# A transformer block on one core: tiles split straight from PSUM, shifts added apart, new orders, and the FFN gating on ScalarE and GpSimd

## The chip, the cores and the metric

The kernel runs on one core of a Trainium2 chip. The metric is the device time of one execution in microseconds. TensorE (PE), VectorE (DVE), ScalarE (ACT) and GpSimd (POOL) work from lists of instructions of their own and wait for each other by semaphores. All loads and stores are issued by SyncE (SP).

## What is computed

Four sequences ("batches") of 512 tokens with 512 features, all in float32:

```python
mod = (silu(c) @ wmod).reshape(4, 6, 1, -1)             # c is (4, 512), wmod (512, 3072)
sa, ca, ga, sb, cb, gb = (mod[:, i] for i in range(6))
ga = (2 * (ga >= 0) - 1) * maximum(abs(ga), 0.25)       # and gb likewise
h = layernorm(x) * (1 + ca) + sa
x = x + ga * attention(h)                               # one head, D = 128: qkv, softmax, Wo, bo
h = layernorm(x) * (1 + cb) + sb
x = x + gb * ffn(h)
# ffn(h): h @ W_up.T, plus, for the first of 4 experts with the largest logit
# (h @ gate_w.T + expert_bias), the rank 8 product lora_B @ (lora_A @ h)
```

## The kernel before

A float32 product is done as three products of two parts: a high part in fp32r and the low rest, hi*lo + lo*hi + hi*hi. `products` (L384) issues such triples. So every operand tile needs two passes: a copy that rounds to the high part, and a subtraction that gives the low part. Each tile is 128 partitions by 512 columns, four to a batch.

**Modulation.** `mod_rows(s)` multiplies the split silu of c with the split weights of section s, `mod_columns(s)` turns the rows into columns (`modT`), for sa, ca, sb, cb. The gates ga and gb stay rows: VectorE floors them (`gate_rows`), they are written to DRAM and read back spread over all partitions (`ga_bc`, `gb_bc`). GpSimd multiplies Wo and bo with ga (`output_weights`, `split_output_weights`, `add_output_bias`).

**A batch.** LN1 on VectorE (`ln1_stats`, `ln1_normalise`) with its reciprocal root on GpSimd; TensorE transposes (`x1_transposes`); ScalarE applies scale and shift into an SBUF tile (`h1_evacuate`) and copies its high part (`h1_high`); VectorE or GpSimd subtracts (`h1_low`). Then `qkv`, `qkv_evacuate`, `qk_low`, `scores`, `maxima`, `softmax`, `p_transposes`, `pt_hi`, `pt_low`, `pv`, `out_projection`, the residual and LN2 (`attention_residual_and_ln2`, `ln2_deviation`, `ln2_normalise`), `x2_transposes`, `h2_evacuate`, `h2_high`, `h2_low`.

**The FFN of batch b-1** fills TensorE while batch b does its softmax. `start_ffn` does gate logits and lora A together with the first two token tiles of W_up, `up(b, t)` the other tiles. The gate part goes back to tokens (`z_to_tokens`), VectorE picks the expert in nine dependent steps on small SBUF tiles (`add_parts`, `choose_expert`, L1085 to L1115), TensorE transposes the masked result (`z_transposes`, L563), and `lora_up` (L573) closes each tile. `gate_ffn` (VectorE, L1125) multiplies the tile with gb out of PSUM, `outputs` (GpSimd, L1333) adds it to x, and SP stores it.

**What sets the order.** Each engine's list is written out by hand at the end of its block. `psum_plan` lists all uses of the eight PSUM banks in three rings; `open_bank` makes TensorE wait until the last reader of the bank's earlier content has finished (`last_read`). SP's list is in order too: a load into a reused buffer waits there (`slot_split`).

In batch 0 the lists are different: TensorE mixes in mod rows of ga, sb, cb, gb and the transposes of gate_w, lora_B and W_up. The last part of its list after scores(0):

```python
scores(0); v_transposes(0); gate_transposes(); lora_b_transposes(); mod_rows("sb", (0, 1))
```

## Time and profile before

| | us |
|---|---|
| median of 3 runs | 217.43 |
| lowest, highest | 215.95, 218.15 |
| span of the profiled execution | 216.5 |
| TensorE busy, 974 matmuls | 189.9 (88%) |
| VectorE busy, 312 instructions | 155.9 (72%) |
| GpSimd busy, 122 instructions | 119.5 (55%) |
| ScalarE busy, 210 instructions | 113.8 (53%) |
| the chain that ended last: TensorE, VectorE, GpSimd | 54%, 24%, 9% |

Busy times are sums over an engine's instructions; matmuls are pipelined, so that one shows as about 0.39 us though the next starts 0.23 us after it. The span is the time from the first to the last instruction of one profiled execution, and the rows below are times from its start. The times of the three runs lie around it.

### The profile page before, as it was taken

Reading aid. Unit: us, or ns where it says so; the run is one execution under the profiler, and the core shown is the slowest. Engines: PE = TensorE matmul, PEld = TensorE weight load, DVE = VectorE, ACT = ScalarE, POOL = GpSimd, SP = SyncE. Lnnn points to the kernel's source line nnn. Section 1 sums busy time; section 2 is a strip of 40 time slices with the busy share of each in tenths; the row PEclk is TensorE's granted clock in tenths of the full one; section 3 lists DMA queues with packets and bytes.
Section 4 is the critical chain, followed back from the end, with each engine's and each line's share of the span. In section 5 each row is a group of like instructions: output and inputs, shape, how many; then the busy total and the mean of one; then the engine's idle time right before and its main releaser. Section 6 shows DMA issues by size and latency. Waiting matters only on the chain.

```text
span 216.5 us, 2939 instructions
## 1 busy us (share of the span) xinstructions
PE 189.9 (88%) x974; PEld 148.0 (68%) x974; DVE 155.9 (72%) x312; ACT 113.8 (53%) x210; POOL 119.5 (55%) x122
## 2 busy tenths in 40 slices
PE   7597799999879999499999999399999984998991
PEld 6437676776637787387888778288887853887870
DVE  0898796997989778974935949858343296899255
ACT  2813966669519885415677734247875421087110
POOL 1619172145978067943793929647938194662014
PEclk9969999999979999969999999979999997999999
DMA  5999849135000052000002060000210700202005
GB/s 166 343 375 261 288 173 362 53 100 191 4 0 0 3 195 97 2 0 3 2 32 113 3 132 13 0 2 0 75 73 0 145 0 3 94 4 97 3 0 194
DMA packets 13454, 19.49 MB, mean 90 GB/s; under 512 B 3920, under 2 KB 4432, under 8 KB 13440
## 3 DMA queue, kind: packets, MB, share of 16 engines
q1 hardware_dynamic: 13440, 19.31, 27.1%
q8 instruction: 8, 0.13, 0.3%
q14 instruction: 6, 0.05, 0.1%
HBM read 15.10 MB, written 4.21 MB: 89 GB/s over the span
## 4 chain that ended last, share of the span: by engine, by line
PE 54%; DVE 24%; POOL 9%; issue 5%; ACT 4%; DMA 2%; POOLq 0%; DVEq 0%; ACTq 0%
PE bank L384 34%; DVE xn L977 3%; POOL xs L1292 2%; POOL h2lo L1325 2%; PE bank L368 2%; PE bank L516 2%; PE bank L508 2%; PE bank L509 2%; PE bank L489 2%; PE bank L573 2%; DMA ga_bc<-gates_dram 2%; DVE alo L1040 1%; PE bank L423 1%; DVE xs L1061 1%; PE bank L462 1%
## 5 line engine op out<-in xcount | busy, mean ns | idle before, releaser
L1325 POOL TENSOR_TENSOR h2lo<-stage,h2hi 128x512 fp32r<-128x512 f32 x12 | 15.1, 1295 | 15.6 <-ACT h2hi L823 15.6
L1292 POOL TENSOR_TENSOR xs<-xs,gabo 128x512 f32<-128x512 f32 x16 | 21.8, 1384 | 0.2
L384 PE MATMUL bank<-alo,wqkv_hi 128*128 128x512 f32 x48 | 19.3, 402 | 1.8 <-DVE alo L1137 1.4
L384 PE MATMUL bank<-ahi,wqkv_lo 128*128 128x512 f32 x48 | 19.0, 395 | 0.0
L384 PE MATMUL bank<-ahi,wqkv_hi 128*128 128x512 f32 x48 | 18.9, 395 | 0.0
L738 ACT ACTIVATE xn_p<-xs,shift,rstd 128x512 f32<-128x512 f32 x16 | 12.7, 814 | 11.5 <-POOL shift L1304 11.3
L1333 POOL TENSOR_TENSOR xs<-xs,f_gb 128x512 f32<-128x512 f32 x12 | 15.4, 1299 | 5.6 <-DVE f_gb L1125 5.6
L1125 DVE TENSOR_TENSOR f_gb<-bank,gb_bc 128x512 f32<-128x512 f32 x12 | 8.0, 687 | 14.5 <-PE bank L573 7.8
L1318 POOL TENSOR_TENSOR alo<-stage,ahi 128x512 fp32r<-128x512 f32 x8 | 10.3, 1292 | 13.7 <-ACT ahi L731 13.7
L384 PE MATMUL bank<-wup_lo,h2hi 128*128 128x512 f32 x40 | 17.6, 440 | 0.0
L384 PE MATMUL bank<-wup_hi,h2hi 128*128 128x512 f32 x40 | 16.5, 414 | 0.0
L384 PE MATMUL bank<-wup_hi,h2lo 128*128 128x512 f32 x40 | 16.2, 406 | 0.0
L1040 DVE TENSOR_TENSOR alo<-bank,ahi 128x512 fp32r<-128x512 f32 x16 | 10.2, 682 | 8.4 <-ACT ahi L802 8.4
L722 ACT ACTIVATE stage<-bank,modT_sa,modT_ca 128x512 f32<-128x512 f32 x12 | 9.3, 775 | 11.3 <-PE bank L423 11.3
L1061 DVE SCALAR_TENSOR_TENSOR xs<-bank,row_inv,xs 128x512 f32<-128x512 f32 x16 | 11.4, 743 | 5.1 <-PE bank L384 4.5
L368 PE MATMUL bank<-ident 128*128 128x128 f32 x82 | 13.3, 320 | 1.5 <-POOL ident L1337 1.5
L1278 POOL TENSOR_TENSOR wo_ga<-wo_raw,ga_bc 128x512 f32<-128x512 f32 x4 | 5.1, 1287 | 16.4 <-DMA ga_bc<-gates_dram 16.4
L977 DVE TENSOR_SCALAR xn<-xs,moments,rstd 128x512 f32<-128x512 f32 x16 | 12.3, 808 | 2.5 <-POOL rstd L1259 2.3
L368 PEld LDWEIGHTS bank<-ident 128*128 128x128 f32 x82 | 12.2, 231 | 1.5 <-POOL ident L1337 1.5
L1032 DVE TENSOR_REDUCE row_max<-bank 128x1 f32<-128x512 f32 x16 | 10.9, 682 | 2.1 <-PE bank L384 2.0
L384 PEld LDWEIGHTS bank<-alo,wqkv_hi 128*128 128x128 f32 x48 | 9.2, 191 | 4.4 <-issue 1.9
L1311 POOL TENSOR_TENSOR h2lo<-stage,h2hi 128x512 fp32r<-128x512 f32 x6 | 8.5, 1433 | 5.2 <-ACT h2hi L767 5.2
(172 smaller groups left out, 556.5 us busy)
## 6 DMA issues: line engine op xcount, KB each, us to landing
out_dram<-xs SPq DMA_DIRECT2D x16, 256.0 KB, 2.1
xs<-in_L_attn_x_dram SPq DMA_DIRECT2D x3, 1024.0 KB, 5.5
stage<-in_L_wmod_dram SPq DMA_DIRECT2D x8, 256.0 KB, 5.0
xs<-in_L_wmod_dram SPq DMA_DIRECT2D x2, 1024.0 KB, 8.4
stage<-in_L_wmod_dram SPq DMA_DIRECT2D x2, 1024.0 KB, 11.5
xs<-in_L_attn_x_dram SPq DMA_DIRECT2D x4, 256.0 KB, 6.0
xs<-in_L_ffn_W_up_dram SPq DMA_DIRECT2D x1, 1024.0 KB, 8.3
ga_bc<-gates_dram SPq DMA_DIRECT2D x4, 256.0 KB, 4.1
```

What stands on the lines that cost most here:

```text
L368: nc.tensor.matmul(dst[:, 0:P], ident[:], ident[:], start=True, stop=True)
L384: mm = nc.tensor.matmul(dst, w, m, start=first and i == 0, stop=last and i == total - 1)
L722: nc.scalar.activation(h1_full_at[b][:, kt, :], at("x1T", b, kt)[:], ACT.Identity, bias=modT["sa"][:, kt, b:b + 1], scale=modT["ca"][:, kt ...
L738: nc.scalar.activation(xn2_p[:, t, :], xs[:, b, t, :], ACT.Identity, bias=shift[:, t:t + 1], scale=rstd[:, 1, t:t + 1]).then_inc(S["xn2_re ...
L977: nc.vector.tensor_scalar(xn1[:, t, :], xs[:, b, t, :], moments[:, 0, t, 0:1], rstd[:, 0, t:t + 1], ALU.subtract, ALU.mult).then_inc(S["xn ...
L1032: nc.vector.reduce_max(row_max[:, t:t + 1], at("S", b, t)[:], AX_X).then_inc(S["max_ready"], 1)
L1040: nc.vector.tensor_tensor(alo[:, :, q], at("PT", b, t)[:].rearrange("p (k q) -> p k q", k=NT), ahi[:, :, q].bitcast(F32), ALU.subtract).th ...
L1061: nc.vector.scalar_tensor_tensor(xs[:, b, t, :], at("Y", b, t)[:], row_inv[:, t:t + 1], xs[:, b, t, :], ALU.mult, ALU.add).then_inc(S["x2_ ...
L1292: nc.gpsimd.tensor_tensor(xs[:, b, t, :], xs[:, b, t, :], gabo[:], ALU.add).then_inc(S["xb_ready"], 1)
L1318: nc.gpsimd.tensor_tensor(alo[:, kt, :], h1_full_at[b][:, kt, :], ahi[:, kt, :].bitcast(F32), ALU.subtract).then_inc(S["h1_lo"], 1)
L1325: nc.gpsimd.tensor_tensor(h2lo[:, kt, :], h2_full_at[b][:, kt, :], h2hi[:, kt, :].bitcast(F32), ALU.subtract).then_inc(S["h2_lo"], 1)
L1333: nc.gpsimd.tensor_tensor(xs[:, b, t, :], xs[:, b, t, :], gated(n), ALU.add).then_inc(S["out_ready"], 1)
```

## The change

The whole block is rewritten; what is computed stays.

- **Split from PSUM.** `h1_high` and `h2_high` are ScalarE copies out of PSUM with the scale column; `h1_low` and `h2_low` are one VectorE instruction each, PSUM times scale minus high part. The SBUF tiles with the full values are gone, and so is GpSimd's part of the subtractions.
- **Shifts apart.** sa and sb are no longer added to each element. `qkv_shift_rows` and `qkv_shift_columns` push sa through Wqkv, giving a bias column per batch (`qb`). `ffn_shift` pushes sb through W_up and the gate weights; the FFN shift rides in 16 spare rows of the lora product (`lbw`, `zst`), the gate shift is the bias of `gz_evacuate`.
- **Gates as columns.** ga and gb are floored as columns and turned back to rows by `gate_to_rows`.
- **Expert choice in PSUM.** `z_to_tokens` is a product with `fold`, which adds the two parts; the small steps of `choose_expert` work in that PSUM bank.
- **FFN gating.** For batches 0 to 2 `gate_ffn` is replaced by `take_ffn`, a ScalarE copy into one of four `f_gb` buffers, and a GpSimd product in `outputs`. Batch 3 keeps the VectorE product (`gate_last_ffn`).
- **LN1's normalisation** of batches 1 to 3 moves from VectorE to GpSimd.
- **Orders.** `psum_plan` is a list of banks for batch 0 and two rings of five and three after it; all engines' lists, SP's too, are new. `gate_and_lora_a` runs before the scores of the next batch.

The core of the diff:

```diff
@@ psum_plan
+        (6, "gateA"), (5, "loraB"),
+        (0, "PT", 0, 0), (1, "PT", 0, 1), (2, "PT", 0, 2), (3, "PT", 0, 3),
+        (6, "mod", "sb"), (7, "qkv", 1, 0), (0, "qkv", 1, 1), (1, "qkv", 1, 2), (5, "modT", "sb"),
...
+        (5, "x2T", 0, 0), (6, "x2T", 0, 1), (4, "x2T", 0, 2), (2, "x2T", 0, 3),
+        (3, "gate_row", "gb"), (5, "fb"), (6, "gzb"), (2, "gz", 0),
...
@@ sync
+            load_first("ca")
...
+            load_first("sa")
...
+                if b + 2 < B:
+                    spread_gate(0, b + 2)
...
@@ tensor
+            mod_rows("ca")
+            keep_warm(bank[4], 3)
+            mod_columns("ca")
+            keep_warm(bank[4], 4)
+            first_x1_transposes()
+            keep_warm(bank[4], 4)
+            qkv(0, (0, 1))
+            mod_rows("sa")
+            qkv(0, (2,))
+            mod_columns("sa")
+            qkv(0, (3,))
+            qkv_shift_rows()
+            mod_rows("ga", (0, 1))
+            qkv_shift_columns()
+            mod_rows("ga", (2, 3))
+            scores(0)
+            v_transposes(0)
+            mod_columns("ga")
+            gate_to_rows("ga")
+            x1_transposes(1)
+            gate_transposes()
+            lora_b_transposes()
+            p_transposes(0)
+            mod_rows("sb")
+            qkv(1, (0,))
+            mod_columns("sb")
+            pv(0)
+            qkv(1, (1,))
+            out_projection(0)
+            mod_rows("cb")
+            w_up_transposes((0, 1))
+            mod_columns("cb")
+            qkv(1, (2,))
+            mod_rows("gb")
+            w_up_transposes((2, 3))
+            mod_columns("gb")
+            x2_transposes(0)
+            gate_to_rows("gb")
+            qkv(1, (3,))
+            ffn_shift()
+            gate_and_lora_a(0)
+            for b in range(1, B):
+                last = b == LAST
+                scores(b)
+                v_transposes(b)
+                if last:
+                    up(b - 1, 0)
+                else:
+                    up(b - 1, 0, (0, 1))
+                    x1_transposes(b + 1)
+                    up(b - 1, 0, (2, 3))
+                z_to_tokens(b - 1)
+                p_transposes(b)
+                up(b - 1, 1)
+                pv(b)
+                z_transposes(b - 1)
+                up(b - 1, 2, (0, 1))
+                out_projection(b)
+                lora_up(b - 1, 0)
+                lora_up(b - 1, 1)
+                up(b - 1, 2, (2, 3))
+                lora_up(b - 1, 2)
+                up(b - 1, 3)
+                lora_up(b - 1, 3)
+                if not last:
+                    qkv(b + 1, (0, 1))
+                    x2_transposes(b)
+                    qkv(b + 1, (2, 3))
+                    gate_and_lora_a(b)
...
@@ scalar
+                    nc.scalar.activation(h1hi[:, kt, :], at("x1T", b, kt)[:], ACT.Copy,
+                                         scale=modT["ca"][:, kt, b:b + 1]).then_inc(S["h1_hi"], 1)
...
+            def take_ffn(b, t):
+                n = NT * b + t
+                act.wait_ge(S["F_psum"], n + 1)
+                if n >= 4:
+                    act.wait_ge(S["out_ready"], n - 3)
+                nc.scalar.activation(f_gb[:, n % 4, :], at("F", b, t)[:], ACT.Copy).then_inc(S["F_taken"], 1)
...
+            mod_row_evacuate("cb")
+            wup_high((0, 1))
+            mod_high("gb")
+            ln2_normalise(0, (0, 1))
+            mod_row_evacuate("gb")
+            ln2_normalise(0, (2, 3))
+            wo_high(1)
+            wup_high((2, 3))
+            h2_high(0)
+            gate_rows_evacuate("gb")
+            qkv_evacuate(1)
...
+                o_high(b)
+                zT_evacuate(b - 1)
+                take_ffn(b - 1, 0)
+                take_ffn(b - 1, 1)
+                ln2_normalise(b, (0,))
+                take_ffn(b - 1, 2)
+                ln2_normalise(b, (1, 2))
+                take_ffn(b - 1, 3)
+                ln2_normalise(b, (3,))
...
@@ vector
+                    nc.vector.scalar_tensor_tensor(h1lo[:, kt, :], at("x1T", b, kt)[:], modT["ca"][:, kt, b:b + 1],
+                                                   h1hi[:, kt, :].bitcast(F32), ALU.mult,
+                                                   ALU.subtract).then_inc(S["h1_lo"], 1)
...
+            h1_low(0)
+            mod_low("sa", (1, 3))
+            mod_low("ga", (1,))
+            split_sa()
+            mod_low("ga", (3,))
+            ln1_stats(1, (0, 1, 2, 3))
+            ln1_moments(1)
+            mod_low("sb", (1, 3))
+            qkv_shift()
+            qk_low(0)
...
+            maxima(0)
+            gate_columns("ga")
+            v_low(0)
+            h1_low(1, (0, 1))
+            pt_low(0, (0, 1))
+            h1_low(1, (2, 3))
+            pt_low(0, (2, 3))
+            dve.wait_ge(S["gzw_hi_ready"], 1)
...
+            wup_low((0, 1))
+            scale_columns("cb")
+            mod_low("gb", (1, 3))
+            wup_low((2, 3))
+            gate_columns("gb")
+            ln1_stats(2, (0, 1, 2, 3))
+            ln1_moments(2)
+            h2_low(0)
+            qk_low(1)
+            ffn_shift_rows()
+            gate_shift()
...
@@ gpsimd
+                    if b < LAST:
+                        pool.wait_ge(S["F_taken"], n + 1)
+                        if t == 0:
+                            pool.wait_ge(gb_bc_in[b % 2], 16 * (b // 2 + 1))
+                        nc.gpsimd.tensor_tensor(f_gb[:, n % 4, :], f_gb[:, n % 4, :], gb_bc[:, b % 2, :],
+                                                ALU.mult).then_inc(S["f_gb_ready"], 1)
+                        pool.wait_ge(S["f_gb_ready"], n + 1)
...
+            mod_low("cb", BY_POOL["cb"])
+            ln2_deviation(0, range(NT))
+            output_weights(1)
+            mod_low("gb", BY_POOL["gb"])
+            split_output_weights(1)
+            ln1_deviation(2)
+            ln1_normalise(2)
+            for b in range(1, B):
+                last = b == LAST
+                add_output_bias(b)
+                if not last:
+                    output_weights(b + 1)
+                ln2_deviation(b, (0, 1))
+                outputs(b - 1, (0,))
+                ln2_deviation(b, (2,))
+                outputs(b - 1, (1,))
+                ln2_deviation(b, (3,))
+                if not last:
+                    split_output_weights(b + 1)
+                outputs(b - 1, (2, 3))
+                if b + 2 < B:
+                    ln1_deviation(b + 2)
+                    ln1_normalise(b + 2)
```

`gateA` is the bank of the transposed gate and lora A weights; `emptied` (the new `last_read`) frees it with `gzw_lo_ready`, and frees an `x2T` bank with `h2_lo`.

## Rows read from the trace of the kernel before

**Rows 1.** The page, busy us (share of the span) xinstructions of each engine.
```profile
PE 189.9 (88%) x974; PEld 148.0 (68%) x974; DVE 155.9 (72%) x312; ACT 113.8 (53%) x210; POOL 119.5 (55%) x122
```

**Rows 2.** Stretches: from:to, length, busy us and instructions by engine, clock, DMA.
```profile
core 0: us, PE busy (x) PEld busy (x) DVE busy (x) ACT busy (x) POOL busy (x), PEclk, DMA share, GB/s
35.03:55.45 20.42, 19.28 (x111) 14.98 (x110) 17.32 (x30) 16.56 (x34) 9.60 (x7) 1.00 0.39 138
55.45:75.40 19.95, 17.68 (x91) 11.71 (x90) 17.71 (x32) 11.79 (x21) 12.86 (x15) 0.91 0.00 1
75.40:117.60 42.20, 39.15 (x195) 31.78 (x194) 30.59 (x64) 24.83 (x44) 27.34 (x27) 0.96 0.16 57
117.60:159.75 42.15, 38.76 (x193) 31.71 (x192) 28.11 (x58) 22.74 (x40) 27.99 (x28) 0.96 0.14 38
159.75:216.50 56.75, 46.62 (x251) 37.42 (x249) 36.30 (x70) 19.62 (x43) 26.73 (x26) 0.96 0.17 52
```

**Rows 3.** The chain that ended last: start, us on the chain, engine, tile, line, count.
```profile
104.63 8.37 PE bank L384 x36
112.99 1.75 PE bank L489 x16
...
140.17 5.04 PE bank L384 x15
```

**Rows 4.** Timeline of TensorE, batch 2: start, us, instruction [idle before <-releaser].
```profile
139.54 0.63 PE L563 MATMUL bank<-ident,zst 128*128 128x128 f32 x4 [3.39 <-DVE zst L1115]
```

**Rows 5.** Timeline of VectorE, choosing experts of batch 1 (columns as before).
```profile
132.25 0.30 DVE L1085 TENSOR_TENSOR zl_tmp<-bank,logit_bias 128x144 f32<-128x144 f32 x1
...
133.88 1.22 DVE L1098 TENSOR_TENSOR z_arg<-z_arg,first_wins 128x16 f32<-128x16 f32 x1
135.12 0.17 DVE L1100 TENSOR_REDUCE z_max<-z_arg 128x4 f32<-128x16 f32 x1
...
138.97 0.42 DVE L1115 TENSOR_TENSOR zst<-zm,zst 128x256 fp32r<-128x256 f32 x1
```

**Rows 6.** Groups by line and shape: busy us, mean ns | idle before, releaser.
```profile
L1292 POOL TENSOR_TENSOR xs<-xs,gabo 128x512 f32<-128x512 f32 x16 | 21.8, 1384 | 0.2
L738 ACT ACTIVATE xn_p<-xs,shift,rstd 128x512 f32<-128x512 f32 x16 | 12.7, 814 | 11.5 <-POOL shift L1304 11.3
L1061 DVE SCALAR_TENSOR_TENSOR xs<-bank,row_inv,xs 128x512 f32<-128x512 f32 x16 | 11.4, 743 | 5.1 <-PE bank L384 4.5 <-POOL xs L1292 0.5
L1301 POOL TENSOR_TENSOR rstd<-var_eps,neg_half 128x1 f32<-128x1 f32 x16 | 8.8, 550 | 3.0 <-DVE var_eps L1075 2.6
L985 DVE TENSOR_TENSOR h2lo<-stage,h2hi 128x512 fp32r<-128x512 f32 x6 | 8.8, 1502 | 0.4 <-ACT h2hi L767 0.4
L802 ACT ACTIVATE ahi<-bank 128x512 fp32r<-128x512 f32 x16 | 8.7, 596 | 4.2 <-PE bank L462 4.2
L1125 DVE TENSOR_TENSOR f_gb<-bank,gb_bc 128x512 f32<-128x512 f32 x12 | 8.0, 687 | 14.5 <-PE bank L573 7.8 <-POOL xs L1333 6.6
L1281 POOL TENSOR_TENSOR gabo<-bo_bc,ga_bc 128x512 f32<-128x512 f32 x4 | 5.8, 1450 | 0.0
L1278 POOL TENSOR_TENSOR wo_ga<-wo_raw,ga_bc 128x512 f32<-128x512 f32 x4 | 5.1, 1287 | 16.4 <-DMA ga_bc<-gates_dram 16.4
L1304 POOL TENSOR_SCALAR shift<-moments,rstd 128x1 f32<-128x1 f32 x16 | 4.5, 280 | 1.6
```

**Rows 7.** Timeline of VectorE, LN2 of batch 0, first two tiles.
```profile
61.64 0.69 DVE L1069 BATCH_NORM_STATS2 stats<-xs 128x6 f32<-128x512 f32 x1
...
62.65 0.68 DVE L1069 BATCH_NORM_STATS2 stats<-xs 128x6 f32<-128x512 f32 x1
```

**Rows 8.** Timeline of TensorE, its last instruction.
```profile
211.26 0.39 PE L573 MATMUL bank<-lbw,zT 128*128 128x512 f32 x1
```

**Rows 9.** The chain that ended last, where the gates go through DRAM.
```profile
41.26 1.40 DMA gates_dram<-gates
42.68 3.40 DMA ga_bc<-gates_dram
```

More of the change, by code:

```diff
@@ L46 @@
 GZ = E + ER
+LAST = B - 1
 LN_EPS = 1e-5
@@ L113, in psum_plan @@
+    place, earlier, holds = {}, {}, [None] * 8
+    for bank, *name in order:
         place[tuple(name)] = bank
@@ L373, in open_bank @@
                 if before is not None:
-                    ready, count = last_read(*before)
+                    ready, count = emptied(*before)
                     pe.wait_ge(S[ready], count)
@@ new lines, in last_x2_transposes @@
+            def last_x2_transposes():
+                b = LAST
+                for t in range(NT):
+                    pe.wait_ge(S["xn2_ready"], NT * b + t + 1)
+                    for kt in range(NK):
+                        dst = open_bank("x2T", b, kt) if t == 0 else at("x2T", b, kt)
+                        mm = nc.tensor.transpose(dst[:, t * P:(t + 1) * P], xn2_p[:, t, kt * P:(kt + 1) * P], ident[:])
+                        if t == NT - 1:
+                            mm.then_inc(S["x2T_psum"], 1)
@@ new lines, in gate_and_lora_a @@
+            def gate_and_lora_a(b):
+                dst = open_bank("gz", b)
+                if b == 0:
+                    pe.wait_ge(S["gzw_hi_ready"], 1)
+                    pe.wait_ge(S["gzw_lo_ready"], 1)
+                for kt in range(NK):
+                    w = gzw[:, kt, :, :].rearrange("p a g -> p (a g)")
+                    pe.wait_ge(S["h2_hi"], NK * b + kt + 1)
+                    nc.tensor.matmul(dst[0:2 * GZ, :], w, h2hi[:, kt, :], start=kt == 0, stop=False)
+                    pe.wait_ge(S["h2_lo"], NK * b + kt + 1)
+                    mm = nc.tensor.matmul(dst[0:2 * GZ, :], w, h2lo[:, kt, :], start=False, stop=kt == NK - 1)
+                mm.then_inc(S["gz_psum"], 1)
@@ new lines, in z_to_tokens, with z_transposes @@
+            def z_to_tokens(b):
+                dst = open_bank("zl", b)
+                if b == 0:
+                    pe.wait_ge(S["fold_ready"], 1)
+                pe.wait_ge(S["gz_ready"], b + 1)
+                for t in range(NT):
+                    mm = nc.tensor.matmul(dst[:, t * GZ:(t + 1) * GZ], gz[:, t * P:(t + 1) * P], fold[:],
+                                          start=True, stop=True)
+                mm.then_inc(S["zl_psum"], 1)
+            def z_transposes(b):
+                dst = open_bank("zT", b)
+                pe.wait_ge(S["zsel_ready"], 2 * b + 1)
+                pe.wait_ge(S["zst_ready"], 2 * (b + 1))
+                for t in range(NT):
+                    mm = nc.tensor.transpose(dst[:, t * P:(t + 1) * P], zst[:, t].bitcast(F32), ident[:])
+                mm.then_inc(S["zT_psum"], 1)
@@ new lines, in _ @@
+            split_sb()
+            inverse_sums(0)
+            mod_low("cb", (1,))
+            o_low(0)
+            mod_low("cb", (3,))
+            residual(0, 0)
+            ln2_moments(0, 0)
+            residual(0, 1)
+            ln2_moments(0, 1)
+            residual(0, 2)
+            ln2_moments(0, 2)
+            residual(0, 3)
+            ln2_moments(0, 3)
+            wup_low((0, 1))
+            scale_columns("cb")
+            mod_low("gb", (1, 3))
+            wup_low((2, 3))
@@ L1221, in _ @@
+            gate_columns("gb")
[5 more added lines that the diff above has]
+            gate_shift()
+            for b in range(1, B):
+                last = b == LAST
+                maxima(b)
+                v_low(b)
+                if not last:
+                    h1_low(b + 1)
+                pt_low(b)
+                choose_expert(b - 1)
+                inverse_sums(b)
                 if b + 2 < B:
@@ new lines, in _ @@
+                residual(b, 1)
+                ln2_moments(b, 1)
+                residual(b, 2)
+                ln2_moments(b, 2)
+                residual(b, 3)
+                ln2_moments(b, 3)
+                if b + 2 < B:
+                    ln1_stats(b + 2, (2, 3))
+                    ln1_moments(b + 2)
+                h2_low(b)
+                if not last:
+                    qk_low(b + 1)
+            choose_expert(LAST)
+            gate_last_ffn(0)
+            gate_last_ffn(1)
```

1171 lines of the change are left out of this document (500 added, 671 removed).

## Prediction

> **What bounds the kernel now.** I read the page's first two parts first: TensorE is busy 190 of 216.5 us, nothing else above 156 [rows 1]. Then a table of stretches, cut at the first matmul of scores(0), out_projection(0), scores(1), scores(2) and scores(3) [rows 2]. Batches 1 and 2 take 42.2 us each, with TensorE busy 39 and its granted clock 0.96 of the higher level. What they need comes from its pace: 36 512-column matmuls in 8.37 us, 0.2325 a slot, and 16 transposes in 1.75, 0.44 for four [rows 3]. A batch has 132 slots (36 qkv, 12 scores, 12 pv, 12 projection, 48 up, 4 lora, 8 gate) and 60 transposes, 30.7 + 6.6, with the two small z groups about 37.7. So 4.5 us of each stage are lost. They lie at one place: z_transposes waited 3.39 us for `zst` in batch 2 [rows 4], and the 15 matmuls behind that wait took 5.04 where the pace gives 3.5 [rows 3]: the idle engine came back at the lower of its two clock levels. What is late is the chain that picks an expert on VectorE, 132.25 to 139.39 [rows 5].
>
> **Steady stages.** The change alters no matmul of a batch, so 37.7 stays. I lay the new order out from the first matmul of scores(b).
>
> TensorE: scores to 2.8, V 3.2, up half, x1T, up half 7.8, zl 8.6, PT 10.4, up 13.2, pv 16.0, zT 16.4, six up slots 17.8, projection 20.6, 22 slots of up and lora 25.7, 18 of qkv 29.9, x2T, the rest 37.7.
>
> VectorE: four maxima, v_low 5.4, four h1_low from PSUM (as the 0.74 of a PSUM tile with a second operand, [rows 6]) 8.8, four pt_low 12.0. Selection: its small products stood at 1.22 us on SBUF while its reduction took 0.17 [rows 5]; in PSUM nine ops at 0.17 to 0.42 with gaps are 2.8 to 3.1. Bounds: 1.9 (nine at 0.21) and the 7.1 of now. I take 3.1, the ops being the reduction's size. It ends at 15.1, zT at 16.0 doesn't wait, o_low ends at 17.5. The z wait is gone.
>
> This is where the Trainium skill speaks ("SBUF — State Buffer", Who interferes with whom): an op of VectorE with two SBUF inputs and one of GpSimd exclude each other for a whole instruction, one with PSUM input doesn't. The 1.22 against 0.17 agrees. By the rule alone the chain would be near its lower bound; the sum would not move, zT being ready early either way.
>
> What is late next is x2T. Projection tile 0 lands at 18.7. Per tile VectorE spends 0.7 on the residual and 1.01 on statistics [rows 6, 7], so the fourth variance is out at 18.7 + 4 x 1.7 = 25.5. GpSimd answers each with 0.55 + 0.28 [rows 6], but its list now has outputs between: product and sum of a tile, 2.6 (two at 1.29 to 1.38, `wo_ga` and `xs`), where it had one op. Second deviation 23.1, output 25.7, third 26.6, output 29.2, fourth 30.1; ScalarE's 0.81 makes 31.0, against TensorE's 29.9. Wait: 1.1. Stage 1: 37.7 + 1.1 = 38.9. In it GpSimd goes on with wo_lo, two outputs (to 38.3), a deviation and the four normalisations that VectorE had. No 512-column tensor_scalar of GpSimd is in this trace; from 0.5 (its 0.28 on one column, doubled) to 1.4 (its two-input ops), I take 1.3, nearest in width. It ends at 44.6, stage 2's x1T wants it at 38.9 + 4.6 = 43.5. Half that wait, for the low end: stage 2 = 39.5.
>
> The Trainium skill ("GPSIMD Engine Reference", Engine selection) has one-input ops near line rate and two-input ones twice VectorE's time. By it normalising would leave no wait and the sum would be 0.6 lower. No run here shows it yet.
>
> The title's edit: VectorE loses four 0.68 a batch, ScalarE gains four 0.60, GpSimd four 1.29. All three stay under 30 of 38.9 us, so it gains nothing by itself; its cost is the 1.1 above, and more in batch 3. Dropping the full-precision SBUF copies of h1 and h2 takes eight ScalarE passes and GpSimd's h_low out of each batch; neither was on the path. New load order and gate spreads: hidden, the loads being issued over 10 us ahead of use.
>
> Batch 3: without x1T and the gate matmuls the projection runs 15.9 to 18.7, fill 23.8. Variances to 23.6; GpSimd, with two outputs between, 28.1; ScalarE 29.0. TensorE stands from about 26 to 29.1. Then whole-tile splits: h2_low 33.1, gate 33.4, up and lora 15.2 with z groups to 48.6 (lower clock 1.5 included, as after the 3.39 wait). The last lora_up starts at 48.4; from its start, 211.26 before [rows 8], to the end 5.2 stays. Together 53.6 against 56.75.
>
> Steady part: 38.9 + 39.5 + 53.6 = 132.0 against 42.2 + 42.15 + 56.75 = 141.1. Gain 9.1.
>
> **Batch 0.** It has new work and, above all, new waits.
>
> (a) To scores(0). First rows normalised 17.5, h1 split 19.7, then TensorE has 36 + 8 + 8 slots, 8 narrower and the columns: 34.0. The q and k bias comes through VectorE, which between split_sa (28.4, when TensorE delivers) and qkv_shift has one ga low, four statistics, moments, two sb lows: 34.5, bias 35.2, two ScalarE passes 36.5. Scores 36.6, end 39.9. Before: start 35.03.
>
> (b) To the projection. Gate columns follow maxima(0): 43.5, x1T, gateA, loraB 46.7, PT 48.5. Now mod("sb") sits in the bank of gateA, free only with gzw_lo_ready, which VectorE gives after the last pt_low: 52.2. Wait 3.7. Then 8 + 9 + 12 + 9 slots and columns, 9.2, and 1.5 of low clock: 62.9. Before: 55.45. Gate DMAs cost 1.40 + 3.40 [rows 9]; from 44.8 wo_ga starts 49.7 and wo_lo is out at 58.3, hidden.
>
> (c) To scores(1). The first residual follows the last cb low, 63.9; fourth variance 70.9, deviation 71.8. GpSimd then does output_weights(1) (2.75) before mod_low("gb"): 74.6, halves at 75.9 and 77.2. TensorE has been ready since 71.0. mod_rows("gb") ends 78.1; ScalarE evacuates it (78.9) before the last two ln2_normalise (80.5), then wo_high, wup_high (82.1); VectorE wup_low, gate_columns (83.8), four statistics and moments of batch 2 (87.1), and only then h2_low, 89.8. ffn_shift waits for the bank of x2T 0 (87.9), gate_and_lora_a starts at 90.1 and ends 92.0. So scores(1) start at 92.0, 16.6 after 75.40. Of that 1.9 is the gate matmuls, moved ahead; the rest is wait. If VectorE's SBUF operands meet GpSimd as `h2lo<-stage` did (1.5 instead of 0.69, [rows 6]), two or three lows add 0.9 each; if hand-overs overlap better, 89. Bounds 88 to 95.
>
> **Sum.** 92.0 + 132.0 = 224.0 against the profiled span 216.5. The median of the runs is 217.4, 0.9 above it: 225 us, slower by 3.5%.
>
> **Rivals.** (B) The gating holds LN2: GpSimd's ops at 1.45 or more (the row of `gabo`, [rows 6]) and VectorE delayed by them; 1.5 more in each of three stages: 229.5. For it: GpSimd's steady load rises to 30 us. Against: three ops a stage lie on that path. (C) Selection stays at 7.1 because the small size, not SBUF, is its cost: zT waits 2.8, o_low behind it 2 to 3 a stage, 4 in the tail: 235. Against it the 0.17 row. (D) No measurable change: (c) is over-counted, 9 late at scores(1) in place of 16.6, all gains as computed: 217.3. (E) Faster: TensorE doesn't stand in batch 0, because banks and lists hand over as fast as it works. Its own work there grows by the narrow q, k, v bias slots 1.4, ffn_shift 2.2 and the gate matmuls 1.9, less 1.9 for eight slots fewer in the gates' rows: 3.6, against some 0.6 that fewer warm-up matmuls return. 216.5 + 3 - 9.1 + 0.9 = 211. It decides once scores(1) start before 82.2. Against it: gzw_lo and mod_low("gb") stand in the lists behind work whose durations are read, not guessed. That the change does nothing is D too.
>
> **How the numbers follow.** Likeliest case 0.50, its own range 219 to 229 (batch 0 between 88 and 95, stages +-1). B 0.11, C 0.07, D 0.17, E 0.15. A measurement here tells 1% from none, 2.2 us. Slower: the likeliest (nearly all of it), B, C: 0.68. Same: D, 0.17. Faster: E, 0.15. Range 214 to 232: it leaves out C, most of E and the edge of B.
>
> **What would show it.** Right: a TensorE idle stretch before mod_rows("sb") released by gzw, one of 4 us or more before mod_rows("gb") released by GpSimd; scores(1) near 92, stages 39 to 40, no wait at z_transposes. Wrong: scores(1) below 84 (D or E), z_transposes waiting (C), stages above 41 with `shift` or a GpSimd row as releaser of x2T (B).

## The result: 237.7 us, slower by 9.4%

| | before | after |
|---|---|---|
| median, us | 217.53 (215.95 to 218.15) | 237.67 (237.34 to 238.45) |
| ratio, 95% interval | 1 | 1.0935 (1.0888 to 1.0983) |
| span of the profiled execution | 216.5 | 236.3 |

All medians here and below leave out executions over 1.5% above the fastest of their kernel, which are one of four of g1 and two of four of g7 (with them the medians are 230.49 and 211.48).

The direction was forecast and the size was not: 225 us with a range of 214 to 232. The page after, its span, the busy time of each engine and the chain that ended last, by engine and line:

```profile
span 236.3 us, 2898 instructions
...
PE 197.4 (84%) x961; PEld 151.3 (64%) x961; DVE 138.4 (59%) x310; ACT 102.1 (43%) x186; POOL 133.6 (57%) x131
...
PE 42%; POOL 27%; DVE 17%; issue 9%; ACT 4%; POOLq 0%; DVEq 0%; ACTq 0%
PE bank L346 21%; POOL xn L1271 9%; POOL xs L1333 4%; POOL f_gb L1328 4%; DVE plo L1048 4%; PE bank L414 4%; DVE xs L1065 3%; DVE stats L1072 3%; PE bank L332 3%; POOL rstd L1303 2%; PE bank L361 2%; PE bank L362 2%; POOL rstd L1258 1%; PE bank L518 1%; POOL h2lo L1313 1%
```

Against [rows 1], VectorE lost 17.5 us and GpSimd gained 14.1; of the chain GpSimd now has 27% (9% before). TensorE has 13 matmuls fewer and is busy 7.5 us longer; the next view shows a granted clock of 0.89 in both halves of batch 0, where it was 1.00 and 0.91 [rows 2].

The same stretches as in [rows 2], cut at the first matmul of scores(0), of the projection of batch 0, of scores(1), scores(2) and scores(3). Columns: from:to, length, busy us and instructions of each engine, granted clock, DMA share, GB/s:

```profile
34.26:64.12 29.86, 21.63 (x106) 16.48 (x107) 17.64 (x36) 14.06 (x29) 20.40 (x14) 0.89 0.17 54
64.12:94.07 29.95, 23.26 (x111) 15.38 (x111) 22.86 (x46) 14.02 (x24) 15.19 (x17) 0.89 0.28 97
94.07:134.90 40.83, 38.27 (x198) 30.90 (x197) 26.53 (x61) 20.07 (x36) 27.57 (x27) 1.00 0.05 20
134.90:181.90 47.00, 40.56 (x198) 33.07 (x197) 22.96 (x51) 20.40 (x36) 31.26 (x29) 0.93 0.09 34
181.90:236.30 54.40, 44.85 (x209) 35.03 (x207) 25.06 (x61) 16.35 (x30) 19.99 (x22) 0.94 0.14 49
```

Set against the milestones of the prediction:

| stretch | forecast | measured | miss |
|---|---|---|---|
| start to scores(0) | 36.6 | 34.26 | -2.3 |
| scores(0) to the first projection | 26.3 | 29.86 | +3.6 |
| the projection to scores(1) | 29.1 | 29.95 | +0.8 |
| stage 1 | 38.9 | 40.83 | +1.9 |
| stage 2 | 39.5 | 47.00 | +7.5 |
| scores(3) to the end | 53.6 | 54.40 | +0.8 |
| span | 224.0 | 236.3 | +12.3 |

Most of the miss is one stage. The view of the waits of TensorE after (line waited for, releaser, us in total, times, longest) says on whom:

```profile
PE bank L414 <- POOL xn L1271: 6.6, 2, 3.9
PE bank L361 <- POOL h2lo L1313: 5.2, 1, 5.2
PE bank L494 <- ACT xn_p L774: 4.0, 2, 2.8
PE bank L346 <- DVE zst L1114: 3.5, 3, 1.2
PE bank L361 <- DVE gzw L1189: 3.4, 1, 3.4
PE bank L485 <- ACT xn_p L774: 2.7, 2, 1.3
```

The second and the fifth line are the two new waits of batch 0 that were forecast. The first is the next batch's x1 transposes waiting for the normalisation that GpSimd took over: 2.65 us in batch 0 and 3.93 in stage 2. The fourth is a wait that the prediction didn't have at all. GpSimd's groups that matter (mean ns after the busy time), from the page:

```profile
L1271 POOL TENSOR_SCALAR xn<-xs,moments,rstd 128x512 f32<-128x512 f32 x12 | 24.8, 2079 | 0.2
L1333 POOL TENSOR_TENSOR xs<-xs,f_gb 128x512 f32<-128x512 f32 x14 | 18.0, 1287 | 12.2 <-DVE f_gb L1123 11.3
L1328 POOL TENSOR_TENSOR f_gb<-f_gb,gb_bc 128x512 f32<-128x512 f32 x12 | 15.5, 1290 | 0.0
```

One normalisation takes 2.08 us. The prediction gave it 1.3 with 1.4 as the most. The gating product costs the 1.29 it was given. This is GpSimd around the start of stage 2 (timeline: start, us, instruction, idle before it):

```profile
127.61 1.27 POOL L1289 TENSOR_TENSOR wo_lo<-wo_ga,wo_hi 128x512 fp32r<-128x512 f32 x1 [1.45 <-ACT wo_hi L793]
128.84 1.30 POOL L1328 TENSOR_TENSOR f_gb<-f_gb,gb_bc 128x512 f32<-128x512 f32 x1
130.22 1.30 POOL L1333 TENSOR_TENSOR xs<-xs,f_gb 128x512 f32<-128x512 f32 x1
131.48 1.29 POOL L1328 TENSOR_TENSOR f_gb<-f_gb,gb_bc 128x512 f32<-128x512 f32 x1
132.85 1.30 POOL L1333 TENSOR_TENSOR xs<-xs,f_gb 128x512 f32<-128x512 f32 x1
134.10 1.03 POOL L1258 TENSOR_TENSOR rstd<-var_eps,neg_half 128x4 f32<-128x4 f32 x1
135.23 8.24 POOL L1271 TENSOR_SCALAR xn<-xs,moments,rstd 128x512 f32<-128x512 f32 x4
```

From 127.61 to 143.47 GpSimd is never idle: product, sum, product, sum, deviation, four normalisations in 8.24 us. TensorE wants the result at 139.6 and gets it at 143.5:

```profile
143.53 0.48 PE L414 MATMUL bank<-ident,xn 128*128 128x128 f32 x1 [3.93 <-POOL xn L1271]
```

### The profile page after: what moved, and what is told of

Read it like the earlier page. It is cut to its first block, busy times and chain, and to the rows that moved or that the text cites. A ratio compares the mean times of both kernels' runs of the same rounds, so it can differ in the third digit from the quotient of the medians.

```text
span 236.3 us, 2898 instructions
## 1 busy us (share of the span) xinstructions
PE 197.4 (84%) x961; PEld 151.3 (64%) x961; DVE 138.4 (59%) x310; ACT 102.1 (43%) x186; POOL 133.6 (57%) x131
## 4 chain that ended last, share of the span: by engine, by line
PE 42%; POOL 27%; DVE 17%; issue 9%; ACT 4%; POOLq 0%; DVEq 0%; ACTq 0%
PE bank L346 21%; POOL xn L1271 9%; POOL xs L1333 4%; POOL f_gb L1328 4%; DVE plo L1048 4%; PE bank L414 4%; DVE xs L1065 3%; DVE stats L1072 3%; PE bank L332 3%; POOL rstd L1303 2%; PE bank L361 2%; PE bank L362 2%; POOL rstd L1258 1%; PE bank L518 1%; POOL h2lo L1313 1%
## 5 line engine op out<-in xcount | busy, mean ns | idle before, releaser
L346 PE MATMUL bank<-wup_hi,h2lo 128*128 128x512 f32 x64 | 25.9, 404 | 0.0
L1271 POOL TENSOR_SCALAR xn<-xs,moments,rstd 128x512 f32<-128x512 f32 x12 | 24.8, 2079 | 0.2
L1019 DVE SCALAR_TENSOR_TENSOR h2lo<-bank,modT_cb,h2hi 128x512 fp32r<-128x512 f32 x16 | 10.9, 743 | 17.5 <-ACT h2hi L786 17.5
L346 PE MATMUL bank<-h1lo,wqkv_hi 128*128 128x512 f32 x48 | 19.5, 406 | 0.4 <-DVE h1lo L1012 0.4
L774 ACT ACTIVATE xn_p<-xs,shift,rstd 128x512 f32<-128x512 f32 x16 | 12.8, 810 | 14.8 <-POOL shift L1306 14.5
L346 PE MATMUL bank<-h1hi,wqkv_hi 128*128 128x512 f32 x48 | 19.0, 395 | 0.0
L346 PE MATMUL bank<-h1hi,wqkv_lo 128*128 128x512 f32 x48 | 18.9, 394 | 0.0
L1012 DVE SCALAR_TENSOR_TENSOR h1lo<-bank,modT_ca,h1hi 128x512 fp32r<-128x512 f32 x16 | 11.4, 747 | 12.2 <-ACT h1hi L693 11.8
L693 ACT ACTIVATE h1hi<-bank,modT_ca 128x512 fp32r<-128x512 f32 x16 | 10.2, 689 | 12.7 <-PE bank L414 8.5
L1328 POOL TENSOR_TENSOR f_gb<-f_gb,gb_bc 128x512 f32<-128x512 f32 x12 | 15.5, 1290 | 0.0
L346 PEld LDWEIGHTS bank<-wup_lo,h2hi 128*128 128x128 f32 x64 | 12.8, 199 | 2.5 <-issue 0.2
L346 PEld LDWEIGHTS bank<-wup_hi,h2hi 128*128 128x128 f32 x64 | 12.4, 194 | 2.9
L346 PEld LDWEIGHTS bank<-wup_hi,h2lo 128*128 128x128 f32 x64 | 12.6, 197 | 2.4
```

The costliest lines, as they stand in the source:

```text
L346: mm = nc.tensor.matmul(dst, w, m, start=first and i == 0, stop=last and i == total - 1)
L774: nc.scalar.activation(xn2_p[:, t, :], xs[:, b, t, :], ACT.Identity, bias=shift[:, t:t + 1], scale=rstd[:, 1, t:t + 1]).then_inc(S["xn2_re ...
L1012: nc.vector.scalar_tensor_tensor(h1lo[:, kt, :], at("x1T", b, kt)[:], modT["ca"][:, kt, b:b + 1], h1hi[:, kt, :].bitcast(F32), ALU.mult, A ...
L1271: nc.gpsimd.tensor_scalar(xn1[:, t, :], xs[:, b, t, :], moments[:, 0, t, 0:1], rstd[:, 0, t:t + 1], ALU.subtract, ALU.mult).then_inc(S["xn ...
L1328: nc.gpsimd.tensor_tensor(f_gb[:, n % 4, :], f_gb[:, n % 4, :], gb_bc[:, b % 2, :], ALU.mult).then_inc(S["f_gb_ready"], 1)
```

## The experiments

Theory 1: after is slow because the rewrite made GpSimd's list the thing that TensorE waits for, first by the price of the normalisation, then by the gating. Rival 2: the waits of banks (the expert choice, `gzw`, gb's rows) cost more than GpSimd. Rival 3: many small orders, none worth much. Each of the first five kernels mends one wait of the kernel after, the sixth undoes the title's edit. Each experiment ran beside the kernel before, whose median was 216.87 to 217.15 there and 217.53 beside the kernel after. The kernel after was not run again, so a difference to its 237.67 is uncertain by about 0.7 us from that alone. "Stage 1" and "stage 2" are scores(1) to scores(2) and scores(2) to scores(3), "the last part" is what follows.

**g1, normalisation to ScalarE.**

```diff
-  nc.gpsimd.tensor_scalar(xn1[:, t, :], xs[:, b, t, :], moments[:, 0, t, 0:1], rstd[:, 0, t:t + 1],
-                          ALU.subtract, ALU.mult)
+  nc.scalar.activation(xn1[:, t, :], xs[:, b, t, :], ACT.Identity, bias=shift1[:, t:t + 1],
+                       scale=rstd[:, 0, t:t + 1])
...
-                outputs(b - 1, (2, 3))
                 if b + 2 < B:
                     ln1_deviation(b + 2)
                     ln1_normalise(b + 2)
+                outputs(b - 1, (2, 3))
```

(GpSimd keeps the small `shift1`, mean times deviation. The second part of the cut is a change of order: GpSimd does the deviation of LN1 ahead of the last two outputs.)

> The changed kernel with one part undone: LN1's normalisation of batches 1 to 3 leaves GpSimd and goes to ScalarE (scale and shift, as LN2's), 0.81 us a tile in place of 2.08. Theory A (the slow GpSimd normalisation is the largest term missed): batch 2's stage, scores(2) to scores(3), falls from 47.0 to about 41, as batch 1's; in batch 0 x1_transposes(1) start at 41 instead of 43.7 and at the higher clock, so scores(1) come 3 to 4 us earlier; together 227 to 228 in place of 237.7. Rival (the wait for xn is only where lateness shows, GpSimd's list being the bound): less than 2 us gained, and the wait reappears at x2_transposes or the projection.

Measured: 229.70 us (229.39 to 231.28), 8.0 less than after and 2 more than expected. Scores(1) start 2.5 earlier, not 3 to 4, since `xn` from ScalarE still keeps TensorE waiting for 1.68 in batch 0. Stage 1 is 41.55, 0.7 longer than after. Stage 2:

```profile
133.08:173.61 40.53, 38.03 (x197) 30.97 (x196) 22.69 (x51) 20.34 (x37) 24.13 (x25) 1.00 0.12 42
```

That is 40.53 instead of 47.00, without a wait on `xn`; ScalarE's instruction takes 0.805 us. A wait of 3.93 removed gave 6.5 in its stage, because the clock came back with it (granted 1.00 instead of 0.93). The two parts of the edit were not run singly, so what the order gave of the 8.0 is open. By an estimate from the rows of the kernel after it gave little: there the deviation ends at 135.13, and four `shift` at 0.26 and four ScalarE instructions at 0.805 behind it would end at 139.4, before the 139.6 at which TensorE asks.

**g2, outputs after all LN2 deviations** in GpSimd's list.

```diff
-  ln2_deviation(b, (0, 1)); outputs(b - 1, (0,)); ln2_deviation(b, (2,)); outputs(b - 1, (1,)); ln2_deviation(b, (3,))
+  ln2_deviation(b, range(NT)); outputs(b - 1, (0, 1))
```

> The changed kernel with GpSimd's outputs behind all four LN2 deviations of a batch, nothing else moved. If the gating's products hold up LN2, the wait of 1.34 us before x2_transposes goes in batches 1 and 2, and the two waits of 1.17 and 2.78 in batch 3 with the low clock behind them: 6 to 7 us off 237.7, stages 39.5, last part 50. Rival (LN2's own chain on VectorE sets x2_transposes): under 1.5 us off.

Measured: 232.91 (231.09 to 233.78), 4.8 less, not the 6 to 7 expected. The waits for `xn_p` in stages 1 and 2 went, stage 1 fell from 40.83 to 39.20 and the last part from 54.4 to 50.3. But stage 2 grew to 47.6, and its wait for `xn` from 3.93 to 5.89. All four outputs stand ahead of the normalisations in either order, and these end at 143.64 (after: 143.47), while TensorE now comes to them 1.8 us earlier. What stage 1 gained, stage 2 gives back: GpSimd's list up to that point is as long as before.

**g3, `choose_expert` ahead of `pt_low`** in VectorE's list, since the bank of O is the one in which the experts are chosen.

```diff
+  choose_expert(b - 1)
   pt_low(b)
-  choose_expert(b - 1)
```

> The changed kernel with VectorE choosing the experts before the four pt_low instead of after. Theory: pv waits 1.16 us in each of three batches for its bank, which the expert choice held until zst; the choice fits in VectorE's idle 1.16 us ahead of pt_low, so pv then waits about 0.4 for the last pt_low: 2 to 2.5 us off in all. Rival (pv waits for pt_low in truth, the release by zst being a coincidence): no gain or a loss of up to 1 us a batch.

Measured: 235.21 (234.62 to 235.5), 2.5 less, and the three waits of 1.16 are gone. As expected.

**g4, gateA's bank emptied before the first half of the probabilities,** on ScalarE and VectorE: the copy to `gzw` is moved ahead of `pt_high(0)`, its low part ahead of `pt_low(0)`.

> The changed kernel with the two instructions that empty the bank of gateA placed before the first pt_high and pt_low of batch 0. Theory: mod_rows(sb) waited 3.43 us for that bank alone, so it starts at 51.0 and everything up to the scores of batch 1 comes 3.0 to 3.4 us earlier. Rival (lateness in batch 0 is set by the gb chain, whatever comes before): the wait moves to pv or to mod_rows(gb) and scores(1) come less than 1 us earlier.

Measured: 233.36 (232.59 to 233.84), 4.3 less; scores(1) start at 90.35 instead of 94.07, 3.7 earlier by a wait of 3.43 removed. The wait doesn't come back elsewhere.

**g5, gb's weights split in `phi` and `plo`,** which are free earlier, and all three engines' lists take them earlier; GpSimd's is shown.

```diff
-  mod_split = {s: (phi, plo) if s in ("ca", "ga") else (h2hi, h2lo) for s in SEQ}
+  mod_split = {s: (phi, plo) if s in ("ca", "ga", "gb") else (h2hi, h2lo) for s in SEQ}
...
+  mod_low("gb", BY_POOL["gb"])
   ln2_deviation(0, range(NT))
   output_weights(1)
-  mod_low("gb", BY_POOL["gb"])
```

> The changed kernel with the split of gb in the phi and plo tiles, which are free after pv(0), so that ScalarE, GpSimd and VectorE can do it before LN2's deviations of batch 0 and output_weights(1). Theory: the wait of 5.21 us before mod_rows(gb), with the low clock behind it (8 matmuls in 3.4 us in place of 1.9), goes; the chain behind it (ScalarE's last two LN2 tiles, W_up's parts, gate columns, statistics, h2_low) then sets, and scores(1) start at 86 to 89 in place of 94.1: 5 to 8 us off 237.7. Rival (the batch is bound by that later chain): scores(1) at 92 or later, under 2 us off.

Measured: 231.36 (230.49 to 232.09), 6.3 less; scores(1) start at 88.35. Both are as expected. A wait of 0.87 for `xn_p` stands where the 5.21 was.

**g6, the title's edit undone** in the kernel after: VectorE multiplies F by gb out of PSUM, GpSimd only adds.

```diff
-  nc.scalar.activation(f_gb[:, n % 4, :], at("F", b, t)[:], ACT.Copy)
-  nc.gpsimd.tensor_tensor(f_gb[:, n % 4, :], f_gb[:, n % 4, :], gb_bc[:, b % 2, :], ALU.mult)
+  nc.vector.tensor_tensor(f_gb[:, n % 4, :], at("F", b, t)[:], gb_bc[:, b % 2, :], ALU.mult)
```

> The changed kernel with the title's edit undone: in batches 0 to 2 VectorE multiplies the FFN tile with gb out of PSUM (two tiles between its LN2 tiles, two after them), ScalarE's copy and GpSimd's product are gone. Theory (GpSimd's list sets batch 2's wait for xn and part of the waits for x2T): GpSimd has 5.2 us less a batch, the 3.93 us wait before x1_transposes(3) goes, the stage falls from 47.0 to 41 or 42, and 5 to 8 us come off 237.7. Rival (VectorE's 0.69 us in the LN2 chain cost as much as GpSimd's products did, and GpSimd's list isn't the bound): within 2 us of 237.7.

Measured: 227.64 (226.63 to 229.95), 10.0 less, more than the 5 to 8 expected and the largest of the single edits. Stage 1 is 39.81 (after: 40.83), stage 2 and the last part (after: 47.00 and 54.40):

```profile
136.79:176.57 39.78, 38.25 (x197) 30.92 (x196) 25.12 (x55) 18.03 (x32) 26.34 (x26) 1.00 0.10 34
176.57:228.00 51.43, 43.72 (x209) 34.19 (x207) 27.51 (x65) 14.29 (x26) 11.03 (x15) 0.97 0.11 42
```

GpSimd's timeline at the same place as shown above:

```profile
129.54 2.53 POOL L1329 TENSOR_TENSOR xs<-xs,f_gb 128x512 f32<-128x512 f32 x2
132.03 1.02 POOL L1259 TENSOR_TENSOR rstd<-var_eps,neg_half 128x4 f32<-128x4 f32 x1
133.16 8.25 POOL L1272 TENSOR_SCALAR xn<-xs,moments,rstd 128x512 f32<-128x512 f32 x4
```

The normalisations take as long (8.25), yet end 4.6 us after scores(2) begin (136.79), not 8.6, and TensorE doesn't wait. Batch 0, in which the edit changes nothing, took 2.9 us longer in this profiled execution, at a lower granted clock (0.77 from 34.86 to 65.00, against 0.89 from 34.26 to 64.12 in the kernel after). The two stages and the last part are together 11.2 shorter. They are shorter where g1 and g2 are: 7.2 in stage 2 (g1: 6.5) and 3.0 in the last part (g2: 4.1).

**h1, the normalisation as one operation instead of two.** This asks where 2.08 us come from. The multiplication by the inverse deviation is left out, so the values are not those of the block; the list and its order are unchanged.

```diff
-  nc.gpsimd.tensor_scalar(xn1[:, t, :], xs[:, b, t, :], moments[:, 0, t, 0:1], rstd[:, 0, t:t + 1], ALU.subtract, ALU.mult)
+  nc.gpsimd.tensor_scalar(xn1[:, t, :], xs[:, b, t, :], moments[:, 0, t, 0:1], None, ALU.subtract)
```

> The kernel after, with GpSimd's LN1 normalisation of batches 1 to 3 as one operation (x minus mean) instead of two (minus mean, times the inverse deviation); the multiplication is left out. Theory 1, the second operation is what makes one instruction take 2.08 us: it falls to 1.1 to 1.4 us, x1T(3)'s wait of 3.93 to under 1.5, x1T(1)'s of 2.65 to under 1, and the time from 237.7 to 229 to 232. Theory 2, the reading of one 128x512 input at GpSimd costs 2 us whatever is done with it: nothing changes. Theory 3, the instruction is shorter but the time falls by less than 3 us, because what follows on GpSimd is late for another cause.

Measured: 231.83 (231.16 to 232.12), 5.8 less. The group on the page:

```profile
L1271 POOL TENSOR_SCALAR xn<-xs,moments 128x512 f32<-128x512 f32 x12 | 18.6, 1568 | 0.2
```

The second operation costs 0.51, and one operation with a column operand still takes 1.57, more than a product of two whole tiles (1.29). The wait for `xn` in stage 2 fell from 3.93 to 1.88, the one in batch 0 went. So theory 1 holds in direction and time (229 to 232), but two of its bounds were too low: 1.4 for the instruction and 1.5 for the wait. Half a microsecond less in each of twelve instructions, in an unchanged list, moved the time by 5.8.

**g7, all five repairs together,** and in batch 0 two moves that no single run has: VectorE takes batch 2's statistics ahead of W_up's second low half, TensorE the last quarter of qkv(1) ahead of `gate_to_rows("gb")`.

> All of it at once: LN1's normalisation on ScalarE, outputs behind the LN2 deviations, expert choice before pt_low, gateA emptied early, gb's split apart; and in batch 0 VectorE does batch 2's statistics before W_up's second low half, TensorE the last quarter of qkv(1) before gate_to_rows(gb). If the waits found are the whole loss, scores(1) start near 83, stages are 38 to 39, the last part 50: 209 us, below the 217 of the kernel before. If each only hides the next, 220 or more.

Measured: 209.70 (208.91 and 210.49), ratio to before 0.965 (0.954 to 0.976), near the 209 expected. The single gains add up to 8.0 + 4.8 + 2.5 + 4.3 + 6.3 = 25.9 us, all together with the two moves gave 28.0. So the waits nearly add up, and rival 3 has it right that no single one makes the kernel slow. Rival 2 isn't refuted as an account of why the kernel is slower than before: the three repairs of bank waits (g3, g4, g5) give 13.1, the two of GpSimd's list (g1, g2) 12.8. But two of the bank waits, 10.6 of the 13.1, were in the forecast, so they don't explain the miss. Its stretches, cut as above from scores(1) on:

```profile
80.75:121.13 40.38, 38.77 (x198) 30.78 (x196) 26.50 (x62) 22.89 (x41) 16.32 (x22) 1.00 0.08 30
121.13:159.29 38.16, 38.01 (x197) 31.06 (x197) 23.20 (x52) 21.32 (x39) 23.71 (x26) 1.00 0.14 47
159.29:208.50 49.21, 43.48 (x209) 34.25 (x207) 25.07 (x61) 16.34 (x30) 22.08 (x23) 0.97 0.16 56
```

TensorE is busy 38.01 of 38.16 us in stage 2: there it hardly waits any more.

**h2, g7 with the title's edit undone.** Is the gating's price its own, or that of the list?

> All repairs of g7 and the gating of batches 0 to 2 back on VectorE, out of PSUM. Theory 1, ScalarE's copy and GpSimd's product cost time of their own also where every wait found so far is mended: 203 to 208 us (g7: 211.5), stages of 38 to 39 us. Theory 2, the ten microseconds of g6 were the same waits that the other repairs take away: 210.5 to 212.5. Theory 3, VectorE, with 12 x 0.69 us more, is now the bound: over 213.

Measured: 212.87 (211.15 to 212.93), ratio to before 0.978 (0.972 to 0.984). Against g7's 209.70 it is no gain and perhaps a loss: the intervals of the two ratios overlap, and g7 has two executions. The time lies between theory 2 (to 212.5) and theory 3 (over 213); theory 1 is refuted. The stages are 40.64 and 38.56, the last part 50.27 (g7: 40.38, 38.16, 49.21). So with all repairs in, the product on GpSimd costs nothing; without them it costs ten (g6). That fits g6, whose gain lay where g1 and g2 find theirs. Which of the repairs takes the cost away was not run.

**b3, the title's edit alone in the kernel before,** with four buffers in a staging tile that is free by then.

> The kernel before with one part of the change alone, the gating of batches 0 to 2 as a ScalarE copy (12 x 0.6 us) and a GpSimd product (12 x 1.29 us) in place of 12 VectorE products out of PSUM. Theory 1, GpSimd's list is what a stage waits for, and the products stand in it ahead of the last batch's LN2 deviations: slower by 2 to 7 us (219 to 224). Theory 2, VectorE's list is what a stage waits for, and the edit takes 2.7 us a stage off it: faster by 2 to 4 (213 to 215). Theory 3, neither: within 1%.

Measured: 219.44 (218.65 to 220.51), ratio 1.012 (1.005 to 1.019): the low edge of theory 1, with an interval that reaches into theory 3. Theory 2 is refuted. Stage 1 is as before (42.21), stage 2 and the last part (before: 42.15 and 56.75) are:

```profile
115.88:158.27 42.39, 38.75 (x194) 31.70 (x193) 26.15 (x54) 24.56 (x44) 33.40 (x33) 0.96 0.14 38
158.27:216.90 58.63, 46.81 (x251) 37.41 (x249) 32.63 (x65) 22.17 (x48) 34.67 (x32) 0.95 0.17 56
```

TensorE still waits for `zst` in both places, 3.64 and 4.38 us. In batch 3 two products and two sums stand ahead of the deviations, and TensorE has a new wait of 1.38 for `xn_p`. That is the effect of the title's edit alone, and it isn't a matter of room: in stage 2 GpSimd is busy 33.40 of 42.39 us here and 31.26 of 47.00 in the kernel after. Here nothing that TensorE waits for in the stage stands behind the products.

**b1, the expert choice in PSUM alone in the kernel before.** The gain of 9.1 in the forecast rested on this part of the change.

```diff
-  nc.vector.tensor_tensor(zl[:], parts[:, :, 0, :], zl_tmp[:], ALU.add)
+  nc.vector.tensor_tensor(parts[:, :, 0, :], parts[:, :, 0, :], zl_tmp[:], ALU.add)
...
-  "zl": ("z_step", Z_STEPS * b + 2)
+  "zl": ("zst_ready", 2 * b + 2)
```

(`zl`, `equal`, `first` and `zm` are slices of the same bank from there on.)

> The kernel before with one part of the change alone: the small tiles of the expert choice lie in the PSUM bank of zl instead of SBUF, same operations otherwise. Theory (the choice was slow because VectorE's SBUF operands met GpSimd): its chain falls from 7.1 to about 3 us, z_transposes in batches 2 and 3 don't wait, 4 to 8 us off 217.4. Rival (the small size or the waits between the steps make it slow): no gain.

Measured: 207.19 (206.23 to 207.97), ratio 0.953 (0.946 to 0.961), the fastest of all. Cut as in [rows 2], the two stages and the last part:

```profile
75.13:117.34 42.21, 39.17 (x195) 31.77 (x194) 30.47 (x64) 24.82 (x44) 27.31 (x27) 0.96 0.15 57
117.34:154.63 37.29, 37.24 (x193) 30.49 (x192) 23.82 (x58) 22.73 (x40) 27.97 (x28) 1.00 0.15 43
154.63:206.00 51.37, 45.35 (x251) 36.21 (x249) 32.35 (x70) 19.55 (x43) 26.64 (x26) 0.99 0.17 57
```

Stage 2 took 37.29 us against 42.15 and the last part 51.37 against 56.75, together 10.2 less. Stage 1 didn't move (42.21). The small steps now (VectorE's timeline; compare [rows 5]):

```profile
133.10 0.18 DVE L1102 TENSOR_TENSOR bank<-bank,first_wins 128x16 f32<-128x16 f32 x1
133.32 0.17 DVE L1104 TENSOR_REDUCE z_max<-bank 128x4 f32<-128x16 f32 x1
...
134.53 0.42 DVE L1119 TENSOR_TENSOR zst<-bank,zst 128x256 fp32r<-128x256 f32 x1
```

The product with `first_wins` took 1.22 before and takes 0.18. From the first of the steps to the last it is 3.0 us (131.99 to 134.95) instead of 7.1. Why the small tiles were slow on SBUF, the kernel before shows by itself. Its choice for batch 3 comes when GpSimd has nothing to do (idle from 197.67 to 210.37), and there the same product on the same SBUF tiles took:

```profile
205.53 0.17 DVE L1098 TENSOR_TENSOR z_arg<-z_arg,first_wins 128x16 f32<-128x16 f32 x1
```

In [rows 5] GpSimd worked throughout, and in b1 too (from 129.49 to 138.39). So neither the small size nor SBUF alone made it slow: it was slow on SBUF beside a working GpSimd, and quick in either of the other two cases.

**b2, b1 and the LN1 normalisation of batches 2 and 3 on ScalarE,** behind the high half of the probabilities, against the wait of 3.01 that stage 1 of b1 keeps (TensorE at z_to_tokens, for `alo`, the low part of the probabilities). The kernel before has the same one:

```profile
91.72 0.47 PE L554 MATMUL bank<-ident,gz 72*128 72x72 f32 x4 [3.01 <-DVE alo L1040]
```

> The kernel before with the expert choice in PSUM (b1, 207.2 us) and the LN1 normalisation of batches 2 and 3 on ScalarE after the hi half of the probabilities. Theory 1, the wait of 3.01 us on alo in stage 1 is VectorE's queue, in which the normalisation (5.7 us) stands ahead of it: stage 1 falls from 42.1 to 39 to 40, the time to 204 to 205.5. Theory 2, x1T of the next batch is then late by as much: 207 as before.

Measured: 210.08 (209.13 to 210.76), 2.9 more than b1. Stage 1 fell only by 1.1, to 41.1, and stage 2 rose by 3.7, to 41.0: the wait for `alo` went, but TensorE waits 1.85 and 1.84 for `xn` from ScalarE, which gets to it late. Both theories missed: the move helps the stage where VectorE was slow, and costs where it wasn't. VectorE's timeline of b1 shows the two, in stage 1 and in stage 2:

```profile
85.11 5.68 DVE L977 TENSOR_SCALAR xn<-xs,moments,rstd 128x512 f32<-128x512 f32 x4 [0.62 <-POOL rstd L1263]
...
125.69 1.92 DVE L977 TENSOR_SCALAR xn<-xs,moments,rstd 128x512 f32<-128x512 f32 x4 [1.71 <-POOL rstd L1263]
```

The same four instructions take 5.68 us and 1.92 us. The columns are as in the timeline of GpSimd above, and x4 means four instructions. In the first case GpSimd has `wo_ga`, `gabo` and two sums under way from 84.97 to 90.50; in the second it is idle from 125.58 to 129.49. The kernel before has the same pair, 5.69 and 1.92.

## Why the prediction was wrong in size

- **The price of GpSimd's normalisation was the main error.** The step that failed: "from 0.5 (its 0.28 on one column, doubled) to 1.4 (its two-input ops), I take 1.3". It measured 2.08. The upper end came from the nearest width, on the thought that two whole inputs are the worst case; an instruction with one whole input and two operations costs more. Four of them are 8.24 instead of 5.2 us, and the wait laid out as 1.1 (44.6 against 43.5), of which half was counted, became 3.93. With 2.08 the prediction's own layout gives 4.2, so the place and the mechanism were right and the term was mis-sized. No low clock was counted behind it, but TensorE came back from it slow (busy 40.56 in stage 2 for the matmuls that took 38.27 in stage 1, clock 0.93 and 1.00): 3.93 + 2.29 is all of the difference between the two stages. In batch 0 it is the wait of 2.65 and sixteen transposes in 3.68 us, where h1, without that wait, took 1.97. h1 is the cleanest price: 0.51 of the 0.78 us by which the instruction was undersized, in an unchanged list, gave 5.8 of the 12.3 missed. Of that 2.7 lie in stage 2 and 3.4 before scores(1), where the granted clock varies between executions. g1, which takes the instruction off GpSimd and also moves two outputs, gave 8.0.
- **A wait on a bank was left out.** The prediction asked whether zT waits, and it doesn't. But O of the batch takes the bank of zl, and the choice, now made inside that bank, releases it. So pv, which stands ahead of zT, waits: 1.16 three times. g3 prices it at 2.5. A tile kept in PSUM holds its bank for as long as the work on it takes, and the plan shows who is next in it.
- **The title's edit was under-priced.** "All three stay under 30 of 38.9 us, so it gains nothing by itself; its cost is the 1.1 above, and more in batch 3." Each of the durations was right (1.29 and 1.29), and GpSimd's busy time stayed under the 30 in stage 1 (27.57) and hardly over it in stage 2 (31.26). But what counts is when the list gets to a certain instruction, not its sum: four products add 5.2 us, part of it ahead of work with a due time. In the kernel after, undoing the edit was worth 10.0 (g6); with the five repairs in, nothing (h2); in the kernel before the edit alone cost 1.2% (b3). Costs that are in series on one list can't be priced apart.
- **The low clock behind waits** was counted at two places, 1.5 each, behind `gzw` in batch 0 and in batch 3. In this execution it stood behind the waits of 2.65, 5.21 and 3.93, behind the 2.78 of batch 3, and not behind the 3.43 of `gzw`: eight matmuls after the 5.21 took 3.4 us, those after the 3.43 took 1.9. Behind the 5.21 the prediction had counted none.
- **Where the 4.5 us of each steady stage were lost was read rightly for one stage of two.** "They lie at one place", at z_transposes, is so in stage 2 and in batch 3 (waits of 3.39 and 4.16). In stage 1 TensorE waited 3.01 at z_to_tokens instead, for `alo`, behind VectorE's normalisation of 5.69 us. So the choice in PSUM alone left stage 1 at 42.21 (b1). That stage 1 fell to 40.83 in the kernel after is not the work of the choice; the likely cause is that VectorE lost the normalisation. In b2, where it goes to ScalarE, the wait for `alo` is gone; that part of the change itself was not run alone.
- **What held.** The bank of gateA: wait forecast 3.7, measured 3.43. gb's rows: 4 or more, measured 5.21, released by GpSimd's `h2lo`. The choice in PSUM: forecast 3.1, measured 2.1 (106.54 to 108.67), with steps of 0.17 to 0.42; no wait at z_transposes. The steady matmul time 37.7: 38.3 in stage 1 (with the low clock 40.6 in stage 2). Batch 0's end 92.0: 94.07, though with two errors of opposite sign, scores(0) 2.3 early and the stretch behind 3.6 long. The last part 53.6: 54.4. b1's gains of 4.9 in stage 2 and 5.4 in the last part are the size that the prediction read as lost.
- **The rivals.** B named the gating and came nearer (229.5), but rested it on dearer products, which came at 1.29, and on LN2; the larger wait was the next batch's x1. C came nearest in time (235), for a wrong cause: the choice took 2.1 us, not 7.1. D and E needed scores(1) before 84; they start at 94.
